# An output product in one-pass high and low parts, and a router by halves under its end

## The chip, the cores and the metric

One NeuronCore of a Trainium2 chip runs the whole program in one launch. The metric is the device time of that launch in microseconds; lower is better.

## The reference, cut to what matters

The reference is a two-layer decoder on x of shape (4, 256, 256), float32. Six blocks follow each other, each `x = x + block(layernorm(x))`. The change touches the end of the second and the beginning of the third:

```
# block 2, latent cross attention: 16 heads over ctx_512 (4, 1601, 64)
attn = softmax(scores); ctx_c = einsum('bhsl,bld->bhsd', attn, kv_r)
x = x + ctx @ Wo.T
# block 3, mixture of 8 experts, top 1, capacity 160
logits = layernorm(x) @ gate_weight.T
top1   = argmax(logits); ranks = cumsum(one_hot(top1)) - 1
dispatch tokens with rank < 160 to their expert, gelu(h w1) w2, weigh by probs
```

The later blocks are a grouped attention, a second cross attention and a second mixture.

## The kernel before, in words

Five instruction streams (TensorE `pe`, ScalarE `act`, VectorE `dve`, GpSimd `pool`, the SyncE DMA queue `sp`) are written by hand, and semaphores order them. Tokens lie as 8 tiles of 128 (`NT`); `X` holds the residual stream. Between stages, `ended(engine, n)` is a barrier of the four compute engines. In most stages PSUM banks go round in the order in which TensorE claims them (`begin`), and a bank is free when its reader has signalled `emptied`.

The third stage is the unit loop of block 2: 32 units `u = (b, p)`, a batch and a pair of heads. In each, TensorE makes turned scores in 13 blocks (`turned_scores`, FRONT of 6 and BACK of 7), the next unit's plain scores (`plain_scores`, two before, two amid and two after), whose maxima VectorE takes (`maxima`, L1489), a short `plain_tail` (VectorE's `tail_maxima`, L1497), and the context. ScalarE exponentiates (L1179), GpSimd adds the weights up (`added_up`, L1904 five times, L1908, L1911), and VectorE divides the context of the unit before by their sums (`normalised`, L1522 and L1525) into `CTX`. Blocks, tail, maxima, keys and sums share three banks in the order `ST_ITEMS`: the third block after the tail takes the tail's bank, when `tail_read` is given.

Each instruction stream is in order. VectorE's order in a unit is: tail maxima, two maxima, `all_maxima`, two maxima, `maximum_rows`, now and then `keys`, `normalised(u - 1)`, two maxima.

The fourth stage multiplies `CTX` by the folded output weights `U`, 8 float32 products of 128x128 with 256 columns for each tile of tokens (`out_product`, key `xo`); VectorE adds the result to `X` and normalises it in halves of four tiles, TensorE turns it (`turn_x(2)`) into `HT`. A barrier follows. The fifth stage waits for all weights of the mixture, turns the gate weights (`g_T`), makes all logits (`logits0`), VectorE chooses (`first_choice`), TensorE ranks (`rank0`), VectorE computes the slots (`f_idx`, L1594). Then GpSimd's indirect DMAs (L1944) scatter the rows into `slot_rows`, SyncE loads them back expert by expert. In the gaps TensorE turns the weights of the next attention (`qkv_weights`, `a_wT`, `a_woT`).

A float32 product is two recorded instructions of TensorE. `split_product` is an existing helper: for each pair of operands it makes three float32r products, high by high, high by low and low by high. The float32r format is used so in the query product (`z_jobs`) and the scores.

## Time and profile before

| | |
|---|---|
| median of 3 runs | 1401.38 us (1399.49 to 1403.59) |
| the profiled execution | 1405.69 us, span 1403.9 us |
| mean granted TensorE clock | 0.946 |
| TensorE busy | 1280.9 us (91% of the span) |
| VectorE, ScalarE, GpSimd busy | 809.9, 615.2, 820.2 us |
| chain that ended last | PE 77%, POOL 6%, DVE 5%, ACT 5%, issue 4% |

Times in the rows are microseconds from the span's start. PE is TensorE, DVE is VectorE, ACT is ScalarE, POOL is GpSimd, SP is SyncE. L481 is the line of the helper `mm`, through which most matmuls are recorded. The chain of waits is followed back from the last instruction to what released it. The time of the profiled execution is 4.3 us above the median, and 1.8 us above its span.

### The profile page before, as it was taken

What the parts mean: (1) busy time and instruction counts of PE and PEld (TensorE: products, weight loads), DVE (VectorE), ACT (ScalarE), POOL (GpSimd) and SP (SyncE); (2) the same over time, 40 slices, a digit from 0 to 9 for tenths busy, and PEclk for the clock granted to TensorE, in tenths of its full rate; (3) what the DMA queues carried; (4) which work ended last, traced back from release to release, by engine and by line L of the source; (5) the groups of instructions that cost most, each with busy time, mean ns of one, the idle gap of its engine ahead of it and who ended that gap; (6) DMA issues with size and microseconds to landing.
All of it is one profiled execution on the core that took longest, in us unless ns stands there. A gap on an engine that the chain in (4) does not pass through costs nothing.

```text
span 1403.9 us, 20138 instructions
## 1 busy us (share of the span) xinstructions
PE 1280.9 (91%) x7051; PEld 832.6 (59%) x7051; DVE 809.9 (58%) x1439; ACT 615.2 (44%) x1643; POOL 820.2 (58%) x747
## 2 busy tenths in 40 slices
PE   7999998999999999999979576998999999989793
PEld 4865545666666666666647563444676884547582
DVE  4756666667666666666623426766666123664443
ACT  3731113454454444444430324887666115771151
POOL 1266005999999999999980534988544003560444
PEclk9999997999999999999989687999999997998897
DMA  8501110000000000000008320000000105200263
GB/s 256 132 9 38 31 38 19 9 8 12 9 8 9 12 9 8 8 13 9 8 1 276 105 62 21 1 0 1 1 1 1 27 0 153 61 2 30 67 141 117
DMA packets 67532, 60.12 MB, mean 43 GB/s; under 512 B 19440, under 2 KB 64392, under 8 KB 66920
## 3 DMA queue, kind: packets, MB, share of 16 engines
q1 hardware_dynamic: 64408, 50.56, 12.9%
q0 software_dynamic: 3024, 8.26, 2.5%
q8 instruction: 58, 0.95, 0.3%
q14 instruction: 42, 0.34, 0.1%
HBM read 40.58 MB, written 9.83 MB: 36 GB/s over the span
## 4 chain that ended last, share of the span: by engine, by line
PE 77%; POOL 6%; DVE 5%; ACT 5%; issue 4%; DMA 1%; another core or an unknown queue 0%; POOLq 0%; DVEq 0%; SPq 0%; ACTq 0%
PE PS L481 71%; PE PS L489 5%; ACT s_sc L1278 2%; POOL PWS L1904 2%; POOL a_m L1964 2%; POOL a_m L1958 2%; DVE s_mx L1689 1%; ACT a_m L1235 1%; POOL slot_rows L1944 1%; DVE pm L1489 1%; DVE HN L1380 1%; PE PS L638 0%; PE PS L675 0%; POOL s_sc L1979 0%
## 5 line engine op out<-in xcount | busy, mean ns | idle before, releaser
L1904 POOL TENSOR_TENSOR PWS<-PWS 128x1024 f32<-128x1024 f32 x160 | 379.2, 2370 | 45.9 <-ACT PWS L1179 26.7
L1489 DVE TENSOR_REDUCE pm<-PS 128x2 f32<-128x1024 f32 x192 | 226.0, 1221 | 106.3 <-PE PS L481 106.1
L1179 ACT ACTIVATE PWS<-PS 128x512 f32<-128x512 f32 (+1 forms) x416 | 212.4, 600 | 79.0 <-PE PS L481 73.9
L481 PE MATMUL PS<-PWS,KVR 128*64 128x256 f32 (+1 forms) x1664 | 185.2, 379 | 0.0
L481 PE MATMUL PS<-QALL,KH 128*128 128x512 f32 (+1 forms) x416 | 181.2, 436 | 0.1
L481 PE MATMUL PS<-QM,KL 68*128 68x512 f32 (+1 forms) x416 | 165.8, 398 | 0.0
L1979 POOL TENSOR_SCALAR s_sc<-s_sc,s_ri 128x128 f32<-128x128 f32 (+1 forms) x256 | 103.9, 425 | 101.3 <-DVE s_ri L1696 101.3
L481 PEld LDWEIGHTS PS<-PWS,KVR 128*64 128x64 f32 (+1 forms) x1664 | 121.0, 137 | 58.6 <-issue 0.2
L481 PEld LDWEIGHTS PS<-QALL,KH 128*128 128x128 f32 (+1 forms) x416 | 77.1, 185 | 76.8 <-ACT PWS L1179 59.1
L1278 ACT ACTIVATE s_sc<-PS,s_nb 128x128 f32<-128x128 f32 (+1 forms) x256 | 104.3, 431 | 3.9 <-DVE s_nb L1692 3.9
L1185 ACT ACTIVATE CTX<-PS 128x256 f32<-128x256 f32 x32 | 12.3, 384 | 194.5 <-PE PS L481 194.5
L1689 DVE TENSOR_REDUCE s_mx<-PS 128x2 f32<-128x512 f32 (+2 forms) x112 | 65.7, 611 | 51.8 <-PE PS L481 51.6
L481 PE MATMUL PS<-KH,QALL 64*128 64x512 f32 (+1 forms) x512 | 89.2, 409 | 4.3 <-DVE pm L1489 3.6
L481 PE MATMUL PS<-a_wT,HT 128*128 128x512 f32 x192 | 90.4, 604 | 0.7 <-ACTq L468 0.7
L481 PEld LDWEIGHTS PS<-QM,KL 68*128 68x128 f32 (+1 forms) x416 | 78.2, 188 | 5.8
L481 PEld LDWEIGHTS PS<-KH,QALL 64*128 64x128 f32 (+1 forms) x512 | 46.6, 190 | 39.5 <-issue 24.8
L481 PE MATMUL PS<-z_HTh,z_w 128*128 128x512 f32 x192 | 67.4, 420 | 2.5 <-DVEq L468 2.5
L2007 POOL DMA_INDIRECT e_x<-token_rows,e_ids x31 | 29.4, 948 | 67.9 <-DVE e_ids L1786 47.4
L1522 DVE RECIPROCAL PS<-PS 128x256 f32<-128x256 f32 x32 | 55.9, 1747 | 21.4 <-PE PS L481 21.4
L1164 ACT ACTIVATE QALL<-PS 64x512 fp32r<-64x512 f32 x32 | 19.0, 592 | 110.1 <-PE PS L481 109.7
L1958 POOL TENSOR_TENSOR a_m<-a_m,a_m 128x512 f32<-128x512 f32 x40 | 50.8, 1271 | 27.3 <-DVE a_m L1666 27.3
L1401 DVE TENSOR_TENSOR X<-X,PS 128x256 f32<-128x256 f32 x40 | 16.8, 419 | 83.3 <-PE PS L481 83.3
(307 smaller groups left out, 2396.4 us busy)
## 6 DMA issues: line engine op xcount, KB each, us to landing
QALL<-qlo SPq DMA_DIRECT2D x32, 128.0 KB, 2.4
QM<-QALL SPq DMA_DIRECT2D x64, 64.0 KB, 2.0
f_w<-in_L_ffn_w_dram SPq DMA_DIRECT2D x2, 2048.0 KB
tile_results<-e_y SPq DMA_DIRECT2D x31, 128.0 KB
a_nat<-in_L_attn_w_qkv_dram SPq DMA_DIRECT2D x1, 3072.0 KB, 22.2
x_wq<-in_L_xattn_Wq_dram SPq DMA_DIRECT2D x1, 2048.0 KB, 10.6
x_wo<-in_L_xattn_Wo_dram SPq DMA_DIRECT2D x2, 1024.0 KB, 7.0
a_wo<-in_L_attn_w_o_dram SPq DMA_DIRECT2D x1, 2048.0 KB, 20.8
```

Source lines behind the costliest of these rows:

```text
L481: return nc.tensor.matmul(o, a, b, start=start, stop=stop, **kw)
L489: last = nc.tensor.transpose(ps[0:w, c:c + r], a, ident[0:r, 0:r])
L1179: nc.scalar.activation(PW[c][0:rows, j * HALF:(j + 1) * HALF], st_bank("block", LT * u + lt)[0:rows, :], ACT.Exp).then_inc(p_ready, 1)
L1278: ins = nc.scalar.activation(s_sc[:, k % 4, h, 0:nk], ps[:, j * nk:(j + 1) * nk], ACT.Exp, bias=s_nb[:, k % 3, h:h + 1], scale=scale, accu ...
L1489: V.tensor_reduce(pm[u % 2][:, :, i // 3, i % 3], src, AX, ALU.max).then_inc(nat_read, 1)
L1522: link(V.reciprocal(sums, sums))
L1689: ins = V.tensor_reduce(s_mx[:, k % 3, i * per:(i + 1) * per], banks.bank(key)[:, 0:per * nk].rearrange("p (h k) -> p h k", h=per), AX, AL ...
L1904: G.tensor_tensor(ACC[:, :], PW[0][:, :] if i == 0 else ACC[:, :], PW[i + 1][:, :], ALU.add).then_inc(acc_step, 1)
L1958: G.tensor_tensor(a_m1[:, n % 6, :], a_m1[:, n % 6, :], a_m2[:, n % 2, :], ALU.add).then_inc(m_sum, 1)
L1964: G.tensor_tensor(m1, m1, a_bt[:, i, s, :].unsqueeze(1).to_broadcast([P, 4, P]), ALU.add).then_inc(qk_ready, 1)
L1979: ins = G.tensor_scalar(s_sc[:, n % 4, h, 0:nk], s_sc[:, n % 4, h, 0:nk], s_ri[:, n % 4, h:h + 1], 1.0, ALU.mult, ALU.mult)
L2007: G.indirect_dma_start(e_x[:, j % 8, :], None, xs1, IndirectOffsetOnAxis(ap=e_ids[:, j:j + 1], axis=0)).then_inc(tile_back[j % 8], 16)
```

## The change

The product of context and output weights is made by `split_product`. VectorE writes the high part of each unit's context (`context_high`, in rows of `QALL` that are read no more) and leaves the low part in place of the context (`CTXL` has the address of `CTX`), at the end of `normalised`. It does the same for a pair of output weights at the end of each of the units 23 to 30 (`weights_split`). The barrier behind the product is gone. TensorE turns the first half of the norm after six tiles, and the gate weights before the last one. Logits and choice are made by halves, with four of the next attention's weight groups turned between them. The sum of the exponentials moves behind `f_idx`. GpSimd starts when the last tile is added and clears `f_yg` after `f_xg`. SyncE loads the expert weights after the slot rows are zeroed, under their own semaphore. The numbers of the later barriers go down by one; the diff leaves them out, and blank lines.

```diff
@@ -171,6 +171,8 @@
         pm = [at(f"pm{i}", 143392 + 128 * i, [P, 2, 2, 4]) for i in range(2)]
         nm = [at(f"nm{i}", 143456 + 32 * i, [P, 4]) for i in range(2)]
         CTX = at("CTX", 151744, [P, PAIRS, B * T])
+        CTXL = at("CTXL", 151744, [P, PAIRS, B * T], F32R)
+        UL = at("UL", 184576, [P, PAIRS, C], F32R)
...
@@ -382,6 +384,9 @@
         acc_step = sem("weights_added_by_pool")
         sum_full = sem("weight_sums_filled")
         norm_done = sem("context_normalised")
+        ch_ready = sem("context_high_parts")
+        uh_ready = sem("output_weights_high_parts")
+        experts_loaded = sem("moe0_expert_weights_loaded")
         mask_ready = sem("expert_choice_ready")
...
@@ -405,6 +410,16 @@
         ADDS = 7
         FRONT, BACK = range(0, 6), range(6, LT)
         CTX_BANK = PS[:, 7 * 512:8 * 512]
+
+        def context_high(b, p):
+
+            return QALL[:, p % 4, b, p // 4, :]
+
+        def weights_high(p):
+
+            return QALL[:, 6, p // 2, p % 2, :] if p < 6 else QALL[:, 7, 0, p % 2, :]
+
+        SPLIT_FROM = 2 * PAIRS + 7
         def keys_due(u):
...
@@ -738,21 +753,29 @@
                     plain_scores(n)
             weight_sums(UNITS - 1)
             ended(pe, 3)
-            for t in range(NT):
-                out_product(("xo", t), [(CTX[:, p, t * P:(t + 1) * P], U[:, p, :]) for p in range(PAIRS)])
-            turn_x(2)
-            ended(pe, 4)
-
-
-            pe.wait_ge(moe0_loaded, 16 * 5)
-            turn(("gT", 0), "act", [g_nat[:, 0:P]])
-            turn(("gT", 1), "act", [g_nat[:, P:C]])
-            pe.wait_ge(*banks.emptied(("gT", 1)))
-            def logits0():
-                ps = begin("logits0", "dve")
-                for t in range(NT):
+            def attended(t):
+
+                b, at_ = t // 2, t % 2 * P
+                ps = begin(("xo", t), "dve")
+                split_product(ps[:, 0:C], [(context_high(b, p)[:, at_:at_ + P], CTXL[:, p, t * P:(t + 1) * P],
+                                            weights_high(p), UL[:, p, :]) for p in range(PAIRS)]).then_inc(filled, 1)
+
+            def turn_half(g):
+
+                pe.wait_ge(hn_ready, NT * 2 + 4 * (g + 1))
+                for kc in range(KC):
+                    turn(("ht", 2, g, kc), "act" if g or kc else "dve",
+                         [HN[2][:, 4 * g + i, kc * P:(kc + 1) * P] for i in range(4)])
+
+            def logits0(g):
+
+                for kc in range(KC):
+                    pe.wait_ge(*banks.emptied(("ht", 2, g, kc)))
+                ps = begin(("logits0", g), "dve")
+                for i in range(4):
+                    t = 4 * g + i
                     for kc in range(KC):
-                        last = mm(ps[:, t * E0:(t + 1) * E0], HT[2][:, kc, t * P:(t + 1) * P], g_T[:, kc, :], kc == 0, kc == KC - 1)
+                        last = mm(ps[:, i * E0:(i + 1) * E0], HT[2][:, kc, t * P:(t + 1) * P], g_T[:, kc, :], kc == 0, kc == KC - 1)
                 last.then_inc(filled, 1)
             def rank0():
...
@@ -791,14 +816,26 @@
                                   it == 0, it == KC - 1)
                 last.then_inc(filled, 1)
-            def qkv_weights(kc):
+            def qkv_weights(kc, groups=range(6)):
                 pe.wait_ge(gqa_loaded, 32)
-                for g in range(6):
+                for g in groups:
                     turn(("awT", kc, g), "act", [a_nat[:, 4 * g + i, kc * P:(kc + 1) * P] for i in range(4)])
-            logits0()
-            qkv_weights(0)
+            for t in range(6):
+                attended(t)
+            turn_half(0)
+            attended(6)
+            pe.wait_ge(moe0_loaded, 16 * 3)
+            turn(("gT", 0), "act", [g_nat[:, 0:P]])
+            turn(("gT", 1), "act", [g_nat[:, P:C]])
+            attended(7)
+            pe.wait_ge(*banks.emptied(("gT", 1)))
+            logits0(0)
+            qkv_weights(0, range(0, 4))
+            turn_half(1)
+            logits0(1)
+            qkv_weights(0, range(4, 6))
             rank0()
...
@@ -1193,13 +1230,18 @@
                     keys(*keys_due(u))
                 context_out(u)
             ended(act, 3)
-            turned_norm(2)
-            ended(act, 4)
+            deviations(2, 0)
+            heads_out(2, 0, 1)
             copy_out(("gT", 0), g_T[:, 0, :], lambda ps: ps[:, 0:E0])
             copy_out(("gT", 1), g_T[:, 1, :], lambda ps: ps[:, 0:E0])
-            for g in range(6):
+            deviations(2, 1)
+            for g in range(4):
+                copy_out(("awT", 0, g), a_wT[:, 0, g * HALF:(g + 1) * HALF])
+            for kc in range(KC):
+                heads_out(2, 1, kc)
+            for g in range(4, 6):
                 copy_out(("awT", 0, g), a_wT[:, 0, g * HALF:(g + 1) * HALF])
             act.wait_ge(e_shift, 1)
...
@@ -1523,6 +1565,16 @@
                 dve.wait_ge(ctx_read, u + 1)
                 out_ = CTX[:, p, b * T:(b + 1) * T]
                 V.tensor_tensor(out_, out_, sums, ALU.mult).then_inc(norm_done, 1)
+                dve.wait_ge(norm_done, u + 1)
+                V.tensor_copy(context_high(b, p), out_).then_inc(ch_ready, 1)
+                dve.wait_ge(ch_ready, u + 1)
+                V.tensor_tensor(CTXL[:, p, b * T:(b + 1) * T], out_, context_high(b, p).bitcast(F32), ALU.subtract)
+
+            def weights_split(p):
+
+                V.tensor_copy(weights_high(p), U[:, p, :]).then_inc(uh_ready, 1)
+                dve.wait_ge(uh_ready, p + 1)
+                V.tensor_tensor(UL[:, p, :], U[:, p, :], weights_high(p).bitcast(F32), ALU.subtract)
             for q in range(4):
                 keys(0, q)
@@ -1551,36 +1603,43 @@
                     normalised(u - 1)
                 for n in after:
                     maxima(n)
+                if SPLIT_FROM <= u < SPLIT_FROM + PAIRS:
+                    weights_split(u - SPLIT_FROM)
             normalised(UNITS - 1)
             ended(dve, 3)
-            turned_norm(2, added("xo"))
-            ended(dve, 4)
+
+            def attended(t):
+                if t == 6:
+                    copy_out(("ht", 2, 0, 0), HT[2][:, 0, 0:HALF])
+                added("xo")(t)
+
+            for g in range(2):
+                normalise(2, g, attended)
             def bcast(a, n):
                 return a.unsqueeze(2).to_broadcast([P, a.shape[1], n])
-            def first_choice(src, E, dst, m):
-
-                link(V.tensor_reduce(f_mx[:, m, :], src, AX, ALU.max))
-                link(V.tensor_tensor(f_v[:, :, 0:E], src, bcast(f_mx[:, m, :], E), ALU.is_equal))
-                link(V.tensor_tensor(f_v[:, :, 0:E], f_v[:, :, 0:E], f_rev[:, :, 0:E], ALU.mult))
-                link(V.tensor_reduce(f_mx[:, 3, :], f_v[:, :, 0:E], AX, ALU.max))
-                link(V.tensor_tensor(dst, f_v[:, :, 0:E], bcast(f_mx[:, 3, :], E), ALU.is_equal))
-
-
-            lg = f_l[:, :, 0:E0]
-            dve.wait_ge(moe0_loaded, 16 * 5)
-            copy_out("logits0", lg, lambda ps: ps[:, 0:NT * E0].rearrange("p (t e) -> p t e", t=NT))
-            dve.wait_ge(*banks.emptied("logits0"))
-            first_choice(lg, E0, f_oh[:, :, 0:E0], 0)
-            V.tensor_tensor(f_b[:, :, 0:E0], lg, bcast(f_mx[:, 0, :], E0), ALU.subtract).then_inc(e_shift, 1)
+            def first_choice(tiles, E, src, dst, m):
+
+                v = f_v[:, tiles, 0:E]
+                link(V.tensor_reduce(f_mx[:, m, tiles], src[:, tiles, 0:E], AX, ALU.max))
+                link(V.tensor_tensor(v, src[:, tiles, 0:E], bcast(f_mx[:, m, tiles], E), ALU.is_equal))
+                link(V.tensor_tensor(v, v, f_rev[:, tiles, 0:E], ALU.mult))
+                link(V.tensor_reduce(f_mx[:, 3, tiles], v, AX, ALU.max))
+                link(V.tensor_tensor(dst[:, tiles, 0:E], v, bcast(f_mx[:, 3, tiles], E), ALU.is_equal))
+
+
+            dve.wait_ge(moe0_loaded, 16 * 3)
             link(V.memset(f_pre[:, 0, :], 0.0))
-            for t in range(1, NT):
-                dve.wait_ge(mask_ready, t - 1) if t > 1 else None
-                V.tensor_tensor(f_pre[:, t, 0:E0], f_pre[:, t - 1, 0:E0], f_oh[:, t - 1, 0:E0], ALU.add).then_inc(mask_ready, 1)
-            dve.wait_ge(e_exp, 1)
-            link(V.tensor_reduce(f_mx[:, 1, :], f_e[:, :, 0:E0], AX, ALU.add))
-            link(V.reciprocal(f_mx[:, 2, :], f_mx[:, 1, :]))
+            for g in range(2):
+                tiles = slice(4 * g, 4 * g + 4)
+                copy_out(("logits0", g), f_l[:, tiles, 0:E0], lambda ps: ps[:, 0:4 * E0].rearrange("p (t e) -> p t e", t=4))
+                dve.wait_ge(*banks.emptied(("logits0", g)))
+                first_choice(tiles, E0, f_l, f_oh, 0)
+                for t in range(1, 5) if g == 0 else range(5, NT):
+                    dve.wait_ge(mask_ready, t - 1) if t > 1 else None
+                    V.tensor_tensor(f_pre[:, t, 0:E0], f_pre[:, t - 1, 0:E0], f_oh[:, t - 1, 0:E0], ALU.add).then_inc(mask_ready, 1)
+            V.tensor_tensor(f_b[:, :, 0:E0], f_l[:, :, 0:E0], bcast(f_mx[:, 0, :], E0), ALU.subtract).then_inc(e_shift, 1)
             ps = banks.take("rank0", "dve")
             rank = ps[:, 0:NT * E0].rearrange("p (t e) -> p t e", t=NT)
             dve.wait_ge(*banks.filled("rank0"))
@@ -1592,6 +1651,9 @@
             link(V.tensor_tensor(f_v[:, :, 0:E0], f_v[:, :, 0:E0], f_oh[:, :, 0:E0], ALU.mult))
             link(V.tensor_reduce(f_slot[:, :], f_v[:, :, 0:E0], AX, ALU.add))
             V.tensor_copy(f_idx[:, :], f_slot[:, :]).then_inc(slots_ready, 1)
+            dve.wait_ge(e_exp, 1)
+            link(V.tensor_reduce(f_mx[:, 1, :], f_e[:, :, 0:E0], AX, ALU.add))
+            link(V.reciprocal(f_mx[:, 2, :], f_mx[:, 1, :]))
             def weigh(key, n, e):
...
@@ -1918,7 +1980,7 @@
                     doubled(n)
                 added_up(u)
             ended(pool, 3)
-            ended(pool, 4)
+            pool.wait_ge(*banks.emptied(("xo", NT - 1)))
             def head_tables(i, s):
                 pool.wait_ge(gqa_bcast, 16 * 6)
@@ -1932,11 +1994,11 @@
                 link(G.tensor_tensor(a_bt[:, i, s, :], a_bt[:, i, s, :], a_tmp[:, s, :], ALU.add))
                 pool.drain().then_inc(tables_ready, 1)
-            G.memset(f_yg[:, :, :], 0.0)
             for e in range(E0):
                 G.memset(f_base[:, e:e + 1], float(e * CAP0))
             G.memset(f_xg[:, :, :], 0.0)
             pool.drain().then_inc(slots_cleared, 1)
+            link(G.memset(f_yg[:, :, :], 0.0))
             last_slot = G.to_reg(SLOTS0 - 1)
             pool.wait_ge(slots_zeroed, 16)
...
@@ -2071,17 +2133,17 @@
             sp.dma_start(g_nat[:, :], L0_ffn_gate_weight).then_inc(moe0_loaded, 16)
             sp.dma_start(f_rev[:, :, :], rev_c).then_inc(moe0_loaded, 16)
             sp.dma_start(f_tri[:, :], tri_c[:, 0:P]).then_inc(moe0_loaded, 16)
-            sp.dma_start(f_w1[:, :, :, :], L0_ffn_w1.rearrange("e (k p) i -> p e k i", p=P)).then_inc(moe0_loaded, 16)
-            sp.dma_start(f_w2[:, :, :, :], L0_ffn_w2.rearrange("e (k p) i -> p e k i", p=P)).then_inc(moe0_loaded, 16)
             sp.dma_start(a_nat[:, :, :], L1_attn_w_qkv.rearrange("(o p) c -> p o c", p=P)).then_inc(gqa_loaded, 16)
             sp.dma_start(a_wo[:, :, :], L1_attn_w_o.rearrange("(o p) k -> p o k", p=P)).then_inc(gqa_loaded, 16)
-            sp.wait_ge(phase_ended, 4 * 4)
+            sp.wait_ge(*banks.emptied(("xo", NT - 1)))
             sp.dma_start(a_cos[:, :, :], cos1_c).then_inc(gqa_bcast, 16)
             sp.dma_start(a_sin[:, :, :], sin1_c).then_inc(gqa_bcast, 16)
             for i, a in enumerate((L1_attn_qn_g, L1_attn_qn_b, L1_attn_kn_g, L1_attn_kn_b)):
                 sp.dma_start(a_gb[:, i, :], a.partition_broadcast(P)).then_inc(gqa_bcast, 16)
             sp.wait_ge(slots_cleared, 1)
             sp.dma_start(xs0.rearrange("(j p) c -> p j c", p=P), f_xg[:, :, :]).then_inc(slots_zeroed, 16)
+            sp.dma_start(f_w1[:, :, :, :], L0_ffn_w1.rearrange("e (k p) i -> p e k i", p=P)).then_inc(experts_loaded, 16)
+            sp.dma_start(f_w2[:, :, :, :], L0_ffn_w2.rearrange("e (k p) i -> p e k i", p=P)).then_inc(experts_loaded, 16)
             sp.wait_ge(rows_sent, 16 * NT)
             for g in range(SLOTS0 // P // 2):
```

## Rows read from the trace of the kernel before

**Rows 1.** Chain of waits, 600 to 900 us: start us, us, what.

```profile
717.34 2.39 POOL PWS L1904
...
735.91 29.79 PE PS L481 x128
...
767.47 1.39 DVE HN L1380 x4
...
771.39 7.00 PE PS L481 x32
...
787.61 0.18 DVE f_idx L1594
```

**Rows 2.** Timeline of one unit: start us, us, engine, line, op, out<-in, count, [idle before].

```profile
634.28 2.36 POOL L1904 TENSOR_TENSOR PWS<-PWS 128x1024 f32<-128x1024 f32 x1
634.36 0.42 DVE L1525 TENSOR_TENSOR CTX<-CTX,PS 128x256 f32<-128x256 f32 x1
...
636.66 2.36 DVE L1489 TENSOR_REDUCE pm<-PS 128x2 f32<-128x1024 f32 x2 [1.87 <-PE PS L481]
636.71 1.28 POOL L1908 TENSOR_TENSOR WS<-PWS 128x512 f32<-128x512 f32 x1
...
639.78 7.42 POOL L1904 TENSOR_TENSOR PWS<-PWS 128x1024 f32<-128x1024 f32 x3 [0.42 <-ACT PWS L1179]
639.83 1.22 PE L481 MATMUL PS<-KH,QALL 128*128 128x66 f32 x8
640.42 0.43 DVE L1497 TENSOR_REDUCE pm<-PS 128x4 f32<-128x260 f32 x1 [1.41 <-PE PS L481]
...
642.02 0.39 PE L481 MATMUL PS<-QALL,KH 128*128 128x512 f32 x1
```

**Rows 3.** Timeline of TensorE in the query product, 102.5 to 104.5 us.

```profile
102.58 0.62 PE L481 MATMUL PS<-z_HTh,z_w 128*128 128x512 f32 x2
...
103.27 0.61 PE L481 MATMUL PS<-z_HTh,z_w 128*128 128x512 f32 x2
```

**Rows 4.** Timeline from the output product to the router, 735 to 790 us.

```profile
741.63 0.42 DVE L1401 TENSOR_TENSOR X<-X,PS 128x256 f32<-128x256 f32 x1 [5.81 <-PE PS L481]
...
765.73 0.42 DVE L1401 TENSOR_TENSOR X<-X,PS 128x256 f32<-128x256 f32 x1 [2.57 <-PE PS L481]
...
778.52 0.22 DVE L1362 COPY f_l<-PS 128x64 f32<-128x64 f32 x1 [8.23 <-PE PS L481]
778.78 0.22 DVE L1564 TENSOR_REDUCE f_mx<-f_l 128x8 f32<-128x64 f32 x1
...
784.14 2.79 PE L489 MATMUL PS<-ident,a_nat 128*128 128x128 f32 x24
...
785.71 3.02 ACT L1065 ACTIVATE a_wT<-PS 128x512 f32<-128x512 f32 x6
```

**Rows 5.** Windows, TensorE: stretch, length, busy (instructions), granted clock, DMA share, GB/s.

```profile
771.40:778.00 6.60, 6.60 (x31) 0.50 0.45 109
```

**Rows 6.** DMA issues, 735 to 800 us: count, KB, us to landing.

```profile
slot_rows<-f_xg SPq DMA_DIRECT2D x1, 1280.0 KB, 6.5
```

**Rows 7.** Timeline at the end of the grouped attention's projections, 968.5 to 970.9 us.

```profile
968.73 1.27 POOL L1958 TENSOR_TENSOR a_m<-a_m,a_m 128x512 f32<-128x512 f32 x1
...
969.40 0.68 DVE L1678 CAST s_maskb<-s_mask 128x128 bf16<-128x128 f32 x1
969.96 1.26 POOL L1964 TENSOR_TENSOR a_m<-a_m,a_bt 128x512 f32<-128x512 f32 x1
970.01 1.30 DVE L1679 CAST s_identb<-ident 128x128 bf16<-128x128 f32 x1
```

**Rows 8.** Timeline beside the scatters, 789 to 795 us.

```profile
789.54 1.49 DVE L1617 TENSOR_TENSOR a_wT<-a_wT,a_mu 128x1280 f32<-128x1280 f32 x1
790.18 1.73 POOL L1944 DMA_INDIRECT slot_rows<-HN,f_idx  x1 [0.31 <-issue]
...
792.22 0.98 POOL L1944 DMA_INDIRECT slot_rows<-HN,f_idx  x1 [0.30 <-issue]
```

More of the change, by code:

```diff
@@ L813, in _ @@
             turn_x(3)
-            ended(pe, 5)
+            ended(pe, 4)
             def qkv(n):
@@ L835, in _ @@
                 qk_turn(n)
-            ended(pe, 6)
+            ended(pe, 5)
             def softmax_units(tag, units, turnable, score, use):
@@ L908, in _ @@
             turn_x(4)
-            ended(pe, 7)
+            ended(pe, 6)
             for ct in range(KC):
@@ L1048, in _ @@
                 shared_down(t)
-            ended(pe, 8)
+            ended(pe, 7)
         @block.scalar
@@ L1221, in _ @@
             ht_out(3)
-            ended(act, 5)
+            ended(act, 4)
             def qk_out(n):
@@ L1254, in _ @@
                     qk_out(n - 4)
-            ended(act, 6)
+            ended(act, 5)
             def softmax_units(tag, units, base_n, scale):
@@ L1295, in _ @@
             turned_norm(4)
-            ended(act, 7)
+            ended(act, 6)
             for ct in range(KC):
@@ L1343, in _ @@
             nc.scalar.activation(f_e[:, :, :], f_e[:, :, :], ACT.Exp).then_inc(e_exp, 1)
-            ended(act, 8)
+            ended(act, 7)
         @block.vector
@@ L1642, in _ @@
             ht_out(3)
-            ended(dve, 5)
+            ended(dve, 4)
             def table(a):
@@ L1679, in _ @@
             V.tensor_copy(s_identb[:, :], ident[:, :]).then_inc(mask_set, 1)
-            ended(dve, 6)
+            ended(dve, 5)
             def softmax_units(tag, units, base_n, scale, after):
@@ L1710, in _ @@
             turned_norm(4, added("ao"))
-            ended(dve, 7)
+            ended(dve, 6)
             def y_after(n, unit):
@@ L1823, in _ @@
                 V.scalar_tensor_tensor(X[:, t, :], e_yg[:, t, 1, :], e_w[:, 1, t:t + 1], X[:, t, :], ALU.mult, ALU.add).then_inc(x_final, 1)
-            ended(dve, 8)
+            ended(dve, 7)
         @block.gpsimd
@@ L1952, in _ @@
                                      bounds_check=last_slot, oob_is_err=False).then_inc(res_back[t], 16)
-            ended(pool, 5)
+            ended(pool, 4)
             def rotated(n):
@@ L1970, in _ @@
                     biased(n - 2)
-            ended(pool, 6)
+            ended(pool, 5)
             G.memset(y_v[:, :, :, :, :], 0.0).then_inc(v_cleared, 1)
@@ L1994, in _ @@
             masked_keys(0)
-            ended(pool, 7)
+            ended(pool, 6)
             masked_keys(1)
@@ L2012, in _ @@
                     G.indirect_dma_start(e_yg[:, t, k, :], None, ys1, IndirectOffsetOnAxis(ap=e_idx[:, k * NT + t:k * NT + t + 1], axis=0)).then_inc(both_back[t], 16)
-            ended(pool, 8)
+            ended(pool, 7)
         @block.sync
```

10 lines of the change are left out of this document (6 added, 4 removed).

## Prediction

> **What bounds the kernel now.** I read the chain of waits first, in order of time. Up to the end of the latent attention it runs through TensorE unit by unit; in the last two units it changes to GpSimd's additions, which run without a break [rows 1]. Then it is TensorE's product of context and output weights (29.8 us for 64 matmuls, recorded as 128 halves), the norm, the router (7.0 us for its logits), and the vector steps that end in `f_idx` at 787.79. Everything up to the next attention waits for `f_idx`. So the change touches two things: the path from the product's start to `f_idx`, 787.79 - 735.91 = 51.9 us long, and the unit loop before it, which gets new work on VectorE and must stay as fast as it is.
>
> Second, I read the timeline of one regular unit, all engines together [rows 2]. The reader should see three facts. VectorE idles between the end of `normalised` (634.36 + 0.42 = 634.78) and the next maxima at 636.66. It idles again before `tail_maxima` at 640.42. And GpSimd hardly idles: one addition of 2.36 us or 1.28 us follows the other with gaps of 0.1 us, and only the first of the next unit, at 639.78, waited 0.42 us.
>
> **The product and the router: what is saved.** A tile's eight float32 products become 24 float32r products of 256 columns. The nearest rows are the split products of 512 columns: three in 103.27 - 102.58 = 0.69 us, 0.23 each [rows 3]; and four products of 66 columns with full 128x128 weights beside four half-height ones in 640.98 - 639.83 = 1.15 us, about 0.12 for each of those with full weights, since little of that is columns [rows 2]. 256 columns at the rate of 512 would be 0.115. I take 0.122 (bounds 0.115 and 0.23), so 2.93 us a tile, against (765.73 - 741.63) / 7 = 3.44 now [rows 4]. Over seven tiles that is 3.6 us. The first tile takes 5.7 us now, the clock still being low; I let it gain 0.8. Against this, eight transposes of 0.116 (0.9) and those of `g_T` (0.3) now stand between the products. The last product ends at start + 26.6 instead of 29.8: **3.1 us saved**.
>
> From the last residual add to the last normalised tile stays 3.1 us (765.73 to 768.86) [rows 1, 4]: start + 29.9. Today follow the barrier, `g_T`, 7.0 us of logits, the choice, and ACT's copies and exponential, for which VectorE waits before it takes the rank. After the change the first half's logits and choice lie beside the second half's norm. ACT then has four `a_wT` copies and two `HT` copies at 0.5 us [rows 4] from start + 29.0 on, so the second half's logits begin at start + 32.2. They are half of 7.0, 3.5 us at the clock that the logits have now (0.50 granted) and 1.8 at the full clock [rows 1, 5]. Copy, five steps of the choice and three sums at 0.25 us or less [rows 4] are 2.2 us; the rank 0.6; the six steps to `f_idx` 1.5. That is start + 38.5 with the full clock and 40.7 with the half one. I take 39.6: **12.3 us saved** in all, 3.1 of them by the product, bounds 11.2 and 13.4; with 0.23 for a product it is 12.3 - 8 x 24 x 0.108 = -8.4, which the overlap of weight loads seen in rows 3 excludes.
>
> What could eat this is off the path. The zeroing of the slot rows lands 6.5 us after its issue [rows 6]; issued at about start + 30, after the memset and six small transfers, it is there at 36.5, two us before `f_idx`. The expert weights (4 MB) follow in the same queue and are wanted only after the rows came back; the eight scatters, which only begin at `f_idx`, take longer than the weights' load. I cost these at nothing; if the weights held up the last scatter, it would be up to 3 us. GpSimd's memset of `f_yg` is moved behind that of `f_xg`, and both lie before `f_idx`. The removed barrier costs nothing more.
>
> **The unit loop: what is added.** Each of 32 units gets a copy (`context_high`) and a subtraction in place (`CTXL`), eight units also both for the output weights. Alone they take an estimated 0.3 us (the copy; one of 64 columns takes 0.22 [rows 4]) and 0.42 (the product with the sums, of the same size [rows 2]). After the last unit they stand in front of the barrier: **0.75 us lost**, with the gaps. In the other units this would fit into the idle 1.9 and 1.4 us.
>
> But they read and write SBUF alone, and the trace shows what happens to such VectorE instructions beside GpSimd. Two casts of 128x128 took 0.68 and 1.30 us and ended at 970.08 and 971.31; the GpSimd additions that they met ended at 970.00 and 971.22 [rows 7]. The casts waited for them, and between the two casts GpSimd got its next addition in. The other way round, the indirect DMA that GpSimd began at 790.18 while VectorE subtracted from SBUF with two SBUF inputs (789.54 to 791.03) took 1.73 us, and the one beside a reduction 0.98 [rows 8]. No row shows a subtraction with two SBUF inputs meeting an addition on GpSimd: its wait lies between nothing and a whole addition of 2.36 us. I take the whole wait, since rows 7 and 8 show the exclusion from both sides.
>
> The Trainium skill (SBUF - State Buffer, section "SBUF: two separate sides") says the same of a vector instruction with two SBUF inputs against a GpSimd one that reads SBUF: whichever starts first keeps the port pair to its end. By that rule the rival below on the unblocked subtraction has no place; rows 7 agree for a copy (0.68 and 1.30 us), and no row shows the subtraction.
>
> Walk through [rows 2], from 634.78. The copy waits for the addition that ends at 636.64, done 636.80. The subtraction finds GpSimd's next addition (1.28 us) running, waits until 638.08 and ends at 638.37; the maxima run 638.4 to 640.76 instead of 636.66 to 639.02. `tail_maxima` was due at 640.42, and the second middle plain product at 640.65 waits for these maxima: 0.1 to 0.2 us of stall at most. Where units are longer by a block of keys there is none. Over the loop I put 1.5 us (0 to 4).
>
> In units 23 to 30 the weights' split comes next, at 640.76. The addition begun at 639.78 runs until 642.16: copy done 642.3. The next addition takes the ports until 644.7; the subtraction ends at 645.0, `tail_maxima` at 645.4. TensorE wants that bank for its third block after the tail, at 642.02: **a stall of 3.45 us**. TensorE is then late and GpSimd is not, so in the next unit its first addition must wait for TensorE's blocks; the copy is ready 0.7 us before it and the pair slips through. So every other unit stalls: those behind splits 0, 2, 4 and 6. The fourth lies in unit 30, where GpSimd already is the chain; I put 2.5 of its 3.45. With 0.25 us for two GpSimd-bound last units: 1.5 + 3 x 3.45 + 2.5 + 0.5 = **14.9 us lost** in the loop.
>
> Sum: -12.3 + 0.75 + 14.9 = **+3.3 us**. The profiled execution took 1405.69 us (span 1403.9, 1.8 around it), 4.3 above the median 1401.38. On the median the forecast is 1404.7 us, or +0.24%. A measurement of this kernel tells apart about 0.3%, 4.2 us.
>
> **Rivals.**
> A. The forecast, waits for both instructions: 1404.7, own range 1399 to 1411. Chance 0.52. About 6 in 10 of it lies within 0.3%, a little over a third above it.
> B. The subtraction does not wait, only the copy. Then a unit's maxima are late by nothing, the weights' copy comes 0.8 us before GpSimd's next addition, and the loop loses 0.4 us: -12.3 + 0.75 + 0.4 = -11.2, so 1390.2 us (-0.8%). Chance 0.30, together with the case that neither waits (1389.8) and with one where only the subtraction does (1 to 3 us more). For it: no row has this pair. Against it: rows 8.
> C. Slower: every split unit stalls. It decides at the 0.7 us by which the copy comes before GpSimd's first addition in the unit after a stall; if the weight copy is later than that, units behind splits 1, 3 and 5 stall as well: 3 x 3.45 = 10.4 more, 1415.0 us (+1.0%). Chance 0.10.
> D. The product saves nothing, since 24 weight loads set its pace at 0.145 or more: 8 x 24 x 0.023 = 4.4 us more on A, 1409.1. Chance 0.08, with the case of late scatters.
>
> **Numbers.** B lies below -0.3%; C and D above +0.3%; A mostly within. Faster 0.30 + 0.02 = 0.32; slower 0.18 + 0.19 = 0.37; same 0.31. The range of 8 in 10 reaches from B to the upper end of A: 1389 to 1411.5; what is left out is C and the tails.
>
> **What would show it.** In the loop: the new copy and subtraction at 1.5 to 2.5 us each instead of 0.3 and 0.42, the copy's end 0.1 us behind the end of an addition; TensorE idle by about 3.4 us behind `tail_maxima` in units 24, 26, 28 and 30; the barrier at about 751 instead of 735.9. If it stands at 737, B is right. Behind it: tile products at 2.9 us, `f_idx` 39 to 41 us behind the product's start. Wrong would make it: another order in which the two engines get the ports, or a product pace off 0.12.

## The result

The changed kernel takes 1422.27 us (median of 5 runs, 1412.05 to 1423.36), the kernel before 1399.77 (5 runs, 1399.49 to 1403.59). The ratio is 1.0133, 95% interval 1.0105 to 1.0161: 1.3% slower (the two medians alone would give 1.6%). The forecast was 1404.7 us and the range ended at 1411.5, so the result lies outside of it. The profiled execution of the changed kernel is its shortest: 1412.05 us, span 1410.3; that of before had 1405.69.

The page of the changed kernel gives busy times and instruction counts:

```profile
PE 1273.9 (90%) x7115; PEld 828.2 (59%) x7115; DVE 920.3 (65%) x1524; ACT 618.1 (44%) x1644; POOL 822.1 (58%) x747
```

VectorE is busy 920.3 us instead of 809.9. Its four new groups of instructions, from the groups by line and shape (busy us, mean ns of one):

```profile
L1569 DVE CAST QALL<-CTX 128x256 fp32r<-128x256 f32 x32 | 46.4, 1450 | 1.1
L1571 DVE TENSOR_TENSOR CTXL<-CTX,QALL 128x256 fp32r<-128x256 f32 x32 | 46.0, 1437 | 1.1
...
L1577 DVE TENSOR_TENSOR UL<-U,QALL 128x256 fp32r<-128x256 f32 x8 | 12.0, 1502 | 0.3
L1575 DVE CAST QALL<-U 128x256 fp32r<-128x256 f32 x8 | 8.5, 1066 | 0.0
```

They are 112.9 us together, where 0.29 and 0.42 us apiece (what the two took at 761.4 and 761.73, beside an idle GpSimd) would be 28. VectorE has idle time in every unit, so this alone costs nothing; what matters is whether TensorE waits. TensorE's waits between 590 and 765 us (what for, us in total, times, longest):

```profile
PE PS L496 <- DVE pm L1539: 12.4, 4, 3.1
PE PS L496 <- POOL WS L1973: 5.2, 1, 5.2
PE PS L496 <- DVEq L483: 3.1, 1, 3.1
```

L496 is the matmul helper (L481 before), L1539 `tail_maxima`. Before, the same stretch has no wait for the maxima. The chain of waits behind the loop, which answers to [rows 1]:

```profile
762.24 19.00 PE PS L496 x144
781.25 0.87 PE PS L504 x8
782.12 2.82 PE PS L496 x24
...
785.16 3.04 PE PS L496 x24
...
790.00 1.32 issue
791.32 2.68 DVE HN L1422 x3
...
794.04 0.67 PE PS L504 x4
794.74 1.09 ACT HT L1102 x2
...
795.92 2.65 PE PS L496 x16
...
804.06 1.20 POOL slot_rows L2006
```

The product starts at 762.24 (735.91 before, [rows 1]) and ends at 788.20, 25.96 us later instead of 29.79. `f_idx` ends at 803.17, 40.93 us behind the product's start instead of 51.88. So the path gave back 10.95 us and the product began 26.3 us later. The second change is in the loop, and I cut the span there. The ends of VectorE's reciprocals of the context sums mark the units; the 23rd and the last of the changed kernel (start us, us, timeline), and then the same two of the kernel before:

```profile
602.17 1.74 DVE L1564 RECIPROCAL PS<-PS 128x256 f32<-128x256 f32 x1
...
759.15 1.77 DVE L1564 RECIPROCAL PS<-PS 128x256 f32<-128x256 f32 x1 [6.09 <-PE PS L496]
```

```profile
601.50 1.74 DVE L1522 RECIPROCAL PS<-PS 128x256 f32<-128x256 f32 x1
...
733.60 1.77 DVE L1522 RECIPROCAL PS<-PS 128x256 f32<-128x256 f32 x1 [10.58 <-PE PS L481]
```

From the end of one to the end of the other, the last nine units take 157.0 us (before 132.1: from 603.24 to 735.37, same marks). Called "late units" below, this stretch is read alike from every profile. The 22 units ahead of it take 347.7 us, before 345.8.

| us | late units | last reciprocal to product | product | product start to `f_idx` |
|---|---|---|---|---|
| before | 132.1 | 0.5 | 29.8 | 51.9 |
| changed | 157.0 | 1.3 | 26.0 | 40.9 |

Late units +24.9, units ahead +1.9, copy and subtraction ahead of the barrier +0.8, path -10.95: +16.7. The first unit came 1.2 us sooner in this profile, so `f_idx` ends 15.4 us later. The spans differ by only 6.4. The stretch from the second cross attention's first score product to the first gather of experts' rows took 131.4 us in this profile and 141.3 in that of before. The granted clock (1.00 is 2.4 GHz, 0.50 is 1.2 GHz) is at 0.50 there for 20.5 us from 1176.7 on and 13.7 us from 1282.5 on in the kernel before, against 3.4 us from 1192.9 on and 6.8 us from 1295.3 on after. No line of the change is there, and the median of the changed kernel's runs is 10 us above its profiled one, so I read the loss from the loop and took those 10 us for chance of that execution. The thirteen profiles of this document bear that out: the stretch takes 131.4 to 141.7 us in them, with a mean granted clock of 0.96 in the shortest and 0.87 in the longest; the changed kernel, run again, has 135.1.

### The profile page after: what moved, and what is told of

Read it like the earlier page. It is cut to its first block and busy times, and to the rows that moved or that the text cites. A ratio compares the mean times of both kernels' runs of the same rounds, so it can differ in the third digit from the quotient of the medians.

```text
span 1410.3 us, 20352 instructions
## 1 busy us (share of the span) xinstructions
PE 1273.9 (90%) x7115; PEld 828.2 (59%) x7115; DVE 920.3 (65%) x1524; ACT 618.1 (44%) x1644; POOL 822.1 (58%) x747
## 5 line engine op out<-in xcount | busy, mean ns | idle before, releaser
L496 PE MATMUL PS<-QALL,KH 128*128 128x512 f32 (+1 forms) x416 | 184.4, 443 | 12.5 <-DVE pm L1539 12.4
L496 PE MATMUL PS<-PWS,KVR 128*64 128x256 f32 (+1 forms) x1664 | 189.0, 385 | 0.0
L496 PE MATMUL PS<-QM,KL 68*128 68x512 f32 (+1 forms) x416 | 169.7, 408 | 0.0
L496 PEld LDWEIGHTS PS<-PWS,KVR 128*64 128x64 f32 (+1 forms) x1664 | 122.0, 140 | 62.8 <-issue 4.9
L496 PEld LDWEIGHTS PS<-QALL,KH 128*128 128x128 f32 (+1 forms) x416 | 78.6, 189 | 87.1 <-ACT PWS L1216 52.2
L1222 ACT ACTIVATE CTX<-PS 128x256 f32<-128x256 f32 x32 | 12.3, 385 | 201.6 <-PE PS L496 201.6
L496 PE MATMUL PS<-KH,QALL 64*128 64x512 f32 (+1 forms) x512 | 91.5, 418 | 5.2 <-DVE pm L1531 4.6
L496 PE MATMUL PS<-a_wT,HT 128*128 128x512 f32 x192 | 91.4, 609 | 0.7 <-ACTq L483 0.7
L496 PEld LDWEIGHTS PS<-QM,KL 68*128 68x128 f32 (+1 forms) x416 | 79.8, 192 | 7.2 <-issue 0.8
L496 PEld LDWEIGHTS PS<-KH,QALL 64*128 64x128 f32 (+1 forms) x512 | 48.4, 192 | 43.0 <-issue 25.8
L496 PE MATMUL PS<-z_HTh,z_w 128*128 128x512 f32 x192 | 67.4, 420 | 2.5 <-DVEq L483 2.5
L1443 DVE TENSOR_TENSOR X<-X,PS 128x256 f32<-128x256 f32 x40 | 16.8, 419 | 78.9 <-PE PS L496 78.7
## 6 DMA issues: line engine op xcount, KB each, us to landing
a_nat<-in_L_attn_w_qkv_dram SPq DMA_DIRECT2D x1, 3072.0 KB, 11.5
x_wq<-in_L_xattn_Wq_dram SPq DMA_DIRECT2D x1, 2048.0 KB, 10.4
```

The costliest lines, as they stand in the source:

```text
L496: return nc.tensor.matmul(o, a, b, start=start, stop=stop, **kw)
```

## The experiments

Ratios are to the kernel before in runs on the same chip. The kernels on the first chip share one set of it (median 1394.42, 23 runs), as do those on the second (1401.47, 27) and the third (1392.94, 15).

**The changed kernel again** (first chip, `a0_again`). No edit.

> The changed kernel once more. Its profiled execution took 1412.05 us and four others 1419.5 to 1423.4. If the difference lies in TensorE's clock in the second cross attention (at 0.50 for some 20 us in the profile before, at full clock in the profile after), a second profile at about 1420 us shows the loop as it was (barrier behind it at 761 us) and a low clock in that stage. If the unit loop itself varies, the barrier's place moves by about 10 us.

Measured: 1411.18 us, ratio 1.0106 (1.0063 to 1.0149); late units 156.6 us, product start to `f_idx` 43.0. The loop repeats; the path gained 8.9 us here instead of 10.95, its logits being at the half clock. No execution of about 1420 us came, so this repeat does not show where those of the result lost their time.

**Weights split behind the loop** (first chip, `e1_splits_last`).

```diff
-                if SPLIT_FROM <= u < SPLIT_FROM + PAIRS:
-                    weights_split(u - SPLIT_FROM)
             normalised(UNITS - 1)
+            for p in range(PAIRS):
+                weights_split(p)
             ended(dve, 3)
```

> The output weights' eight splits behind the last unit, where GpSimd is idle. Theory (the splits in units 23 to 30 stall TensorE four times by 3 us, and the clock falls after each stall): the loop gets back 24.9 us and pays 8 x 0.75 = 6.0 us in front of the barrier, so about 1403 us. Rival (the loss comes from the context splits that every unit has, or is spread over the loop): no less than 1418 us.

Measured: 1390.5 us, 0.9981 (0.9954 to 1.0008); late units 132.5, and 6.6 us from the last reciprocal to the product. All 24 us of the late units come from the weights' splits, though the same work is done, 5.3 us of it now in the open. The expected 1403 us took off from 1422.27, as the 1395 of the next experiment do; from the repeat on this chip, 1411.18, the same subtractions give 1392.3 and 1384.4, 1.8 and 4.8 us above what was measured.

**Context product in PSUM** (first chip, `e2_from_psum`). The normalised context is written over the sums in PSUM, and copy and subtraction read it there. The weights are split where the change has them.

```diff
-                out_ = CTX[:, p, b * T:(b + 1) * T]
-                V.tensor_tensor(out_, out_, sums, ALU.mult).then_inc(norm_done, 1)
-                dve.wait_ge(norm_done, u + 1)
-                V.tensor_copy(context_high(b, p), out_).then_inc(ch_ready, 1)
+                link(V.tensor_tensor(sums, CTX[:, p, b * T:(b + 1) * T], sums, ALU.mult))
+                V.tensor_copy(context_high(b, p), sums).then_inc(ch_ready, 1)
                 dve.wait_ge(ch_ready, u + 1)
-                V.tensor_tensor(CTXL[:, p, b * T:(b + 1) * T], out_, context_high(b, p).bitcast(F32), ALU.subtract)
+                V.tensor_tensor(CTXL[:, p, b * T:(b + 1) * T], sums, context_high(b, p).bitcast(F32), ALU.subtract).then_inc(norm_done, 1)
```

> The normalised context is written in place over the sums in PSUM; its copy and its subtraction read PSUM, so neither has two SBUF inputs nor two-port mode. The weights' splits stay where they are. Theory (waits for the shared port): copy and subtraction take 0.42 us each beside GpSimd's additions, a unit's last maxima end at 4.2 us behind the product with the sums instead of 5.7, so the weights' copy comes before GpSimd's next addition and its subtraction too; no stalls of 3 us are left. 1422 - 24.9 - 1.9 = about 1395 us. Rival (VectorE simply has too much work in these units): the work is 0.1 us a unit more than before, so it stays at 1422 us or above.

Measured: 1379.56 us, 0.989 (0.986 to 0.9921); late units 133.2. The timeline of one of its units (GpSimd's additions run from 658.21 to 665.58 without a break):

```profile
658.21 7.37 POOL L1964 TENSOR_TENSOR PWS<-PWS 128x1024 f32<-128x1024 f32 x3
...
664.18 0.43 DVE L1566 TENSOR_TENSOR PS<-CTX,PS 128x256 f32<-128x256 f32 x1
664.64 0.42 DVE L1567 CAST QALL<-PS 128x256 fp32r<-128x256 f32 x1
665.10 0.42 DVE L1569 TENSOR_TENSOR CTXL<-PS,QALL 128x256 fp32r<-128x256 f32 x1
...
668.75 0.28 DVE L1573 CAST QALL<-U 128x256 fp32r<-128x256 f32 x1
669.06 0.42 DVE L1575 TENSOR_TENSOR UL<-U,QALL 128x256 fp32r<-128x256 f32 x1
669.60 7.43 POOL L1964 TENSOR_TENSOR PWS<-PWS 128x1024 f32<-128x1024 f32 x3 [1.30 <-ACT PWS L1216]
```

Copy and subtraction take 0.42 us each beside a running addition, since one operand is in PSUM. So the unit's next maxima start 2.3 us behind the start of the multiplication instead of 3.8 (603.94 to 607.77 in the changed kernel), and the weights' split, still from SBUF, slips in ahead of GpSimd's next addition. In one unit it does not: a weights' subtraction meets an addition and takes 2.61 us, and TensorE waits 0.7 us, its only wait for `tail_maxima`. The stalls of 3.1 us go without any work being moved or taken out.

**Router alone** (first chip, `e4_router_only`). Float32 product, no copies or subtractions, but the router by halves without barrier.

```diff
-                split_product(ps[:, 0:C], [(context_high(b, p)[:, at_:at_ + P], CTXL[:, p, t * P:(t + 1) * P],
-                                            weights_high(p), UL[:, p, :]) for p in range(PAIRS)]).then_inc(filled, 1)
+                out_product(("xo", t), [(CTX[:, p, t * P:(t + 1) * P], U[:, p, :]) for p in range(PAIRS)])
...
```

> Only the second part of the change: the product stays float32 and nothing is split, the router goes by halves without the barrier. From the product's start to the slots the changed kernel takes 40.9 us (51.9 before), 3.8 of the gain by the product. Theory (all else is kept to the end): 44.8 us here, and the time is 1399.8 - 7.1 = 1392.7 us. Rival (the gain is given back behind the slots, by the expert weights' later load or a low clock): about 1399.8 us.

Measured: 1389.37 us, 0.9952 (0.9926 to 0.9979), as expected; but product start to `f_idx` is 47.2 us, not 44.8. The float32 product takes 31.3 us here, 1.5 more than before, since the transposes now stand between its tiles; so the split product saves 5.4 us against it (25.96), and not 3.8. The other 0.9 us is the second half's logits, 3.57 us at the half clock against 2.65.

**Product alone** (second chip, `e3_product_only`). Copies, subtractions and three-part product of the change, with the old router and its barrier; the expert weights still load behind the zeroing. The cuts are from the difference to the changed kernel.

```diff
+            for t in range(NT):
+                attended(t)
+            turn_x(2)
+            ended(pe, 4)
...
+            logits0()
+            qkv_weights(0)
```

> Only the first part of the change: the splits in the loop and the product from them; the router and its barriers as before (the expert weights load behind the slot rows' zeroing, since the high parts lie where they go). Theory (parts add up): the loop loses 1.9 us in its first 23 units and 24.7 in its last nine, 1.2 in front of the barrier, the product gives back 3.8: before + 24.0 us, ratio 1.017. Rival (the parts hang together, for instance by the clock): within 10 us of before.

Measured: 1422.25 us, 1.0166 (1.0123 to 1.0209); late units 156.4, TensorE's waits for `tail_maxima` 12.2 us in 4. The two halves add up: +1.66% and -0.48% make +1.2%, where the whole change has +1.33% and +1.06%. The loss is the product's alone, the router is a gain.

**Weights' subtractions behind the loop** (second chip, `e5_lows_last`). The copies stay in the units, the eight subtractions move.

```diff
                 V.tensor_copy(weights_high(p), U[:, p, :]).then_inc(uh_ready, 1)
+
+            def weights_low(p):
+
                 dve.wait_ge(uh_ready, p + 1)
...
             normalised(UNITS - 1)
+            for p in range(PAIRS):
+                weights_low(p)
```

> The copies of the output weights stay in units 23 to 30, their subtractions go behind the last unit. Theory (a stall needs two waits in a row): the copy alone ends 7.56 us behind the product with the sums, 0.3 us after TensorE's need of the tail's bank less the maxima's 0.43, so units 24, 26, 28 and 30 stall by 0.8 us at most, the clock doesn't fall, and the last nine units take 132 to 136 us (157 in the changed kernel); 8 x 0.45 = 3.6 us more in front of the barrier. Changed kernel - 18 to - 21 us. Rival (one wait is enough): the last nine units stay above 145 us.

Measured: 1398.0 us, 0.9976 (0.9948 to 1.0005); late units 134.4. TensorE's waits, and a unit with the copy alone:

```profile
PE PS L496 <- DVE pm L1539: 1.5, 4, 0.4
```

```profile
614.81 9.92 POOL L1971 TENSOR_TENSOR PWS<-PWS 128x1024 f32<-128x1024 f32 x4 [0.30 <-ACT PWS L1216]
615.55 1.79 DVE L1575 CAST QALL<-U 128x256 fp32r<-128x256 f32 x1
617.26 0.42 DVE L1539 TENSOR_REDUCE pm<-PS 128x4 f32<-128x260 f32 x1
...
617.73 0.50 PE L496 MATMUL PS<-QALL,KH 128*128 128x512 f32 x1 [0.41 <-DVE pm L1539]
```

One waiting instruction leaves 0.4 us of stall; it takes two in a row to make 3.1. The granted clock stays at 1.00 from 600 to 737 us, past all four waits.

**Stalls filled** (second chip, `e8_stalls_filled`). The changed kernel with 13 products of 512 columns more in each unit that stalls, into a bank whose content is written over afterwards. The edit leaves the waits of the changed kernel as they are and adds work, behind a wait for `ctx_read` that holds nothing up (TensorE has no gap there).

```diff
+        FILLED = (24, 26, 28, 30)
...
                 for lt in blocks:
+                    if lt == 8 and u in FILLED:
+                        pe.wait_ge(ctx_read, u)
+                        for _ in range(13):
+                            mm(CTX_BANK, KH[b % 2][:, 0:P], QALL[:, 7, 3, :, :], True, True, skip_group_check=True)
```

> The changed kernel, and in units 24, 26, 28 and 30, in front of the block that stalls, 13 products of 512 columns more (3.0 us), whose result is written over. Theory (half of the loss is TensorE's clock, which falls after the stall): the stalls stay as long, but the clock stays at 1.00, and the last nine units take 132 + 4 x 3.1 + about 1 = 146 us instead of 157: changed kernel - 11 us, with more work. Rival (the rest of the loss is the engines' queues finding back into step): 157 us, no gain, or a loss of up to 12 us where the products are not covered.

Measured: 1407.53 us, 1.0062 (1.004 to 1.0084); late units 144.9. With 52 matmuls more, the late units are 12.1 us shorter than in the changed kernel. TensorE's granted clock (stretch, length, busy, clock, DMA share, GB/s) around the first two stalls, changed kernel first:

```profile
608.00:612.00 4.00, 3.81 (x19) 1.00 0.00 0
612.00:616.00 4.00, 1.10 (x5) 1.00 0.00 0
616.00:620.00 4.00, 4.00 (x12) 0.50 0.05 11
620.00:624.00 4.00, 4.00 (x25) 0.64 0.10 22
...
648.00:652.00 4.00, 1.26 (x6) 1.00 0.00 0
652.00:656.00 4.00, 3.65 (x12) 0.70 0.00 0
656.00:660.00 4.00, 4.00 (x18) 0.50 0.17 37
```

and the kernel with the stalls filled:

```profile
608.00:616.00 8.00, 8.00 (x38) 1.00 0.00 0
616.00:624.00 8.00, 7.93 (x54) 1.00 0.07 16
648.00:656.00 8.00, 7.92 (x42) 1.00 0.07 16
656.00:664.00 8.00, 8.00 (x60) 1.00 0.00 0
```

With each wait TensorE loses its 2.4 GHz and has 1.2 (granted 0.50) for 6.8, 6.8, 10.2 and 6.8 us. In three of the stalls the clock falls about 1 us after the wait has ended, in the third during the wait (686.7 to 689.9, fall at 687.7). Filled, it stays at 1.00. Since only the waiting is gone and the same blocks are late by the same amount, 12.1 us of the late units' 24.9 were the clock's.

**High parts of the weights by ScalarE** (second chip, `e6_scalar_highs`). The version with the context product in PSUM, and ScalarE copies the weights' high parts.

```diff
+                if SPLIT_FROM <= u < SPLIT_FROM + PAIRS:
+                    p = u - SPLIT_FROM
+                    nc.scalar.activation(weights_high(p), U[:, p, :], ACT.Copy).then_inc(uh_ready, 1)
                 context_out(u)
```

> Context parts from PSUM as in the second experiment, and the weights' high parts copied by ScalarE, in its idle time in front of the context's copy; VectorE only subtracts. Theory: the one subtraction that still waited 2.6 us (unit 26's tail 0.9 us late) does so no more, the last nine units take 132.2 us (133.2): 1 us less than the second experiment, about 0.988 of before. Rival: the subtraction now comes earlier and meets the addition in front; it waits in every unit, but for one addition of 1.3 us only, so no loss either; only above 135 us would the theory be wrong.

Measured: 1388.58 us, 0.9917 (0.989 to 0.9944); late units 132.05, as before the change. Against the version without the edit (133.2) it saves 1.2 us of the loop, which the ratios don't tell apart.

**Zeroing later** (third chip, `e9_zeroing_later`). The chain above has `HN` at 2.68 us for three tiles, and the timeline of the changed kernel shows GpSimd's clearing beside it:

```profile
778.99 1.38 DVE L1422 TENSOR_SCALAR HN<-X,mv,rstd 128x256 f32<-128x256 f32 x4
...
789.02 2.23 POOL L1999 MEMSET f_xg<- 128x2560 f32 x1
789.96 4.03 DVE L1422 TENSOR_SCALAR HN<-X,mv,rstd 128x256 f32<-128x256 f32 x4
791.40 1.80 POOL L2001 MEMSET f_yg<- 128x2048 f32 x1 [0.15 <-issue]
```

```diff
-            pool.wait_ge(*banks.emptied(("xo", NT - 1)))
+            pool.wait_ge(hn_ready, NT * 3)
...
-            link(G.memset(f_yg[:, :, :], 0.0))
...
+            link(G.memset(f_yg[:, :, :], 0.0))
             for n in range(4):
                 head_tables(n // 2, n % 2)
```

> The changed kernel, in which GpSimd begins to clear slot rows when the second half's norm is done, not when the last residual add is, and clears `f_yg` behind the scatters. In the changed kernel's profile the second half's four normalised tiles took 4.03 us where the first half's took 1.38, while GpSimd cleared `f_xg` and `f_yg`. If GpSimd's memsets hold VectorE back there, the four tiles take 1.4 us and `f_idx` comes 2.65 us sooner after the product's start, about 38 us instead of 40.55 at the full clock. The first scatter then waits for the zeroing, issued about 2.3 us later than now, so it gains less, 1 to 2.65 us. Rival: the four tiles are slow for another reason (their own operands or the clock), and stay at about 4 us. The loop is unchanged (late units 156 to 157 us); the time is 0.0 to 0.2% below the changed kernel's, which its ratio will hardly show; the profile decides.

Measured: 1404.34 us, 1.0082 (1.0054 to 1.0109); late units 156.7. The four tiles now take as long as those of the first half:

```profile
785.60 1.39 DVE L1422 TENSOR_SCALAR HN<-X,mv,rstd 128x256 f32<-128x256 f32 x4
796.57 1.39 DVE L1422 TENSOR_SCALAR HN<-X,mv,rstd 128x256 f32<-128x256 f32 x4
```

From the last residual add's start to the norm's end it is 3.1 us again (794.83 to 797.96), and 7.9 to the second half's logits, against 10.4 in the changed kernel and 11.7 in its repeat. `f_idx` comes 39.4 us behind the product's start, where about 38 were expected; the logits now wait for ScalarE's four copies of `a_wT` (797.00 to 799.06). The first scatter comes 40.25 us behind the product's start, 1.6 sooner than in the changed kernel. The theory of the memsets holds, and the rival, a norm that is slow by itself, falls.

**Both together** (third chip, `e10_psum_zeroing_later` beside `e11_psum_again`).

> The version with the context product in PSUM (the two further passes read PSUM), and the later zeroing. Expected: the norm's second half at 1.4 us, the first scatter 1 to 2.65 us sooner after the product's start than in the version without the later zeroing, the loop as in that version (late units 132 to 134 us), and a ratio to the kernel before of about 0.988, 0.001 to 0.002 below that version beside it. If the zeroing becomes the wait, the two are equal.

> The version with the context product in PSUM once more, on the same chip as the one with the later zeroing. Expected ratio 0.989 as before, 0.986 to 0.993; the second half's norm 4.0 us.

Measured: with the later zeroing 1378.97 us, 0.9902 (0.9872 to 0.9931), without it 1381.89, 0.9916 (0.9889 to 0.9944). From the product's start to the first scatter it is 39.35 us (775.54 - 736.19) against 44.0 (779.71 - 735.67), 4.7 us sooner where 1 to 2.65 were expected. The norm's 2.65 us of these are shown (1.38 against 4.03); 1.6 of the remaining 2 us lie in the second half's logits, 3.55 us at the half clock in one profile and 1.92 at the full clock in the other. The scatter's releaser is a new one:

```profile
775.54 1.20 POOL L2003 DMA_INDIRECT slot_rows<-HN,f_idx  x1 [7.07 <-DMA slot_rows<-f_xg]
```

It starts 1.07 us behind the end of `f_idx` instead of 0.89, so the zeroing has no slack left. The ratios of the two don't differ by more than their intervals; the gain is shown by the profiles alone.

## Why the prediction was wrong, point by point

**Which instructions wait: right.** Both passes of a split wait until an addition of GpSimd has ended. Walked from 634.78, the forecast had the copy done after 2.0 us and the subtraction after 3.6; in the unit of 603.94 they are done 2.0 and 3.5 us after the multiplication, and the weights' pair after 7.5 and 10.2, as walked. The rows (timeline of the changed kernel):

```profile
604.40 1.96 DVE L1569 CAST QALL<-CTX 128x256 fp32r<-128x256 f32 x1
606.28 1.28 POOL L1970 TENSOR_TENSOR WS<-PWS 128x512 f32<-128x512 f32 x1
606.39 1.46 DVE L1571 TENSOR_TENSOR CTXL<-CTX,QALL 128x256 fp32r<-128x256 f32 x1
...
609.36 7.37 POOL L1966 TENSOR_TENSOR PWS<-PWS 128x1024 f32<-128x1024 f32 x3 [0.36 <-ACT PWS L1216]
610.04 1.86 DVE L1575 CAST QALL<-U 128x256 fp32r<-128x256 f32 x1
611.93 2.58 DVE L1577 TENSOR_TENSOR UL<-U,QALL 128x256 fp32r<-128x256 f32 x1
614.43 0.42 DVE L1539 TENSOR_REDUCE pm<-PS 128x4 f32<-128x260 f32 x1
614.90 0.50 PE L496 MATMUL PS<-QALL,KH 128*128 128x512 f32 x1 [3.10 <-DVE pm L1539]
```

The reader sees the alternation: at 611.90 the copy ends, GpSimd's second addition (three of 2.46 us each follow from 609.36 on) gets in, and the subtraction that needs the copy waits nearly all of it. By the section of the Trainium skill that the prediction cites (SBUF - State Buffer, "SBUF: two separate sides") the subtraction has to wait; these rows agree, with 2.58 us against 0.42. Rival B (the subtraction doesn't wait) falls with them.

**Which units stall: right.** Four waits, 12.4 us, the longest 3.1; the forecast had 3 x 3.45 + 2.5 = 12.9 in units 24, 26, 28 and 30. Rival C (every split unit stalls) didn't come: the times between the reciprocals are 20.2, 17.2, 20.2, 17.4, 21.1 and 16.8, long and short in turn.

**What a stall costs: the failed step.** "So every other unit stalls", the prediction says, and puts down "a stall of 3.45 us" for each, as if TensorE went on at its old pace afterwards. The late units lost 24.9 us, 12.0 more than the 12.9 (11.5 more with the 0.5 that was put for the last two units). The kernel with the stalls filled shows where they are: 12.1 us vanish when TensorE has work during the wait, since the granted clock then stays at 1.00 instead of falling to 0.50 for 6.8 to 10.2 us. The times between its reciprocals are 18.95, 15.51, 18.99, 15.57, 18.96, 15.52 and 16.55 us: each stalled unit is 3.4 us longer than before, as forecast (the fourth too, where I put 2.5), and the others are as before. In the changed kernel the same are 20.24, 17.21, 20.15, 17.37, 21.13, 16.81 and 17.99: what lies between the two rows is the clock. The prediction weighed the clock in the product and in the logits (0.50 there before [rows 5]) and left it out of the loop, where before it is 1.00 from 240 to 729 us. With the 12.1 us of the filled kernel the forecast would have been 1404.7 + 12.1 = 1416.8, above the range and 5.5 us below the measured median.

**The regular units and the last pair: right.** The 22 units ahead lose 1.9 us (forecast 1.5 for the loop). Ahead of the product 0.8 us are lost (1.33 - 0.55), 0.75 forecast.

**The product: right.** Forecast 3.1 us saved, measured 3.8 (29.79 - 25.96), with tiles at 2.82 and 3.04 us where 2.93 were put. Rival D (24 weight loads set a dearer pace) falls.

**The router: short by one unseen wait.** 12.3 us were to be saved, bounds 11.2 and 13.4; it was 10.95, and 8.9 in the repeat. "From the last residual add to the last normalised tile stays 3.1 us": it became 5.8 (788.21 to 793.99), because GpSimd starts its clearing when the last tile is added, and the norm's passes over SBUF wait for both memsets. The experiment with the later zeroing takes these 2.65 us away. Without the product's part the router saved 7.1 us (10.95 - 3.83) where 9.2 were put. I had moved GpSimd's work in the text and costed it at nothing without asking what VectorE does in those microseconds, though the rule was in my hands two paragraphs further on. Half of the 2 us between 10.95 and 8.9 is the clock of the logits: the 16 matmuls of the second half take 2.65 us in one profile and 3.57 in the other; most of the rest is the product, which ends 25.96 and 26.8 us behind its start.

One sum of the prediction is also off by itself: its terms up to `f_idx` (32.2, the logits' 1.8 or 3.5, then 2.2, 0.6 and 1.5) make 38.3 and 40.0, not 38.5 and 40.7. With them the router's term would have been about 12.7 us and the forecast about 1404.3.

**The later load of the expert weights: right.** It was costed at nothing. From the first scatter to the first turned rows it is 17.6 us (804.06 to 821.69) against 17.3 before (788.67 to 805.94).

**What stays open.** The parts that the profile shows add up to +16.7 us, while the medians differ by 22.5 us here and by 16.8 in the repeat; where the 5.8 us more of the first set of runs lie is not shown. The medians of the changed kernel differ by 11 us between the two sets of runs (1422.3 and 1411.2) while the ratios overlap, and its profiled execution was 10 us below its own median. The stretches at 0.50 in the later stages differ from run to run (above: 20.5 and 3.4 us in the second cross attention); what decides them I didn't test.

## What to carry to other kernels

Before a copy or a subtraction over SBUF is put on VectorE beside a busy GpSimd, give it an operand in PSUM, or cost it at up to one GpSimd instruction of waiting; two dependent ones cost two, since GpSimd gets in between them. A wait of TensorE inside a saturated stretch is to be priced at about twice its length when the clock falls with it: here four of 3.1 us cost 24.9 us, 6.2 each, while four of 0.4 us at most, with the clock at 1.00, cost 2.3 us together. When GpSimd is released earlier, read what VectorE does at that moment.

## What the runs showed of the hardware that was not expected

- The granted clock fell to 0.50 behind a wait of 3.1 us in a loop that had run at 1.00 from 240 to 615 us: the wait ended at 614.90, the fall came at 616.0, and lasted 6.8 us. Waits of 0.4 us, and one of 0.7, left it at 1.00. A 512-column product went from 0.40 us to 0.63 there.
- More work made the late units shorter: 52 more products, 12.1 us less.
- A copy of 128x256 took 0.42 us from PSUM beside a running GpSimd addition, and 1.8 to 2.0 us from SBUF in the units shown (1.45 in the mean of 32), where it takes 0.29 alone.
- GpSimd's memset, which reads nothing, also held back VectorE's normalising passes, whose tensor operand and result are in SBUF: 4.03 us for four instead of 1.38.
